# Mamba layer of a 12-layer kernel: projection in two halves, convolution halves in banks of their own, absolute value by ScalarE, the gate's Silu after the exponentials, last states in three pieces

## The chip, the cores and the metric
One core of a Trainium2 chip runs the whole program. The metric is the device time in microseconds, median of 3 runs. Engines: TensorE (PE; its weight loads are PEld), VectorE (DVE), ScalarE (ACT), GpSimd (POOL), SyncE (SP). Each has its own instruction queue, executed in order; they meet by semaphores.

## The reference, cut to what matters
The program is a stack of four groups of three layers on x of shape (2, 128, 256). The change touches the second layer only, a Mamba layer (b = 2, l = 128, 256 channels, 16 states, a convolution over 4 steps):

```python
xz = layernorm(x) @ W_in                      # 256 -> 512
xc, r = jnp.split(xz, 2, axis=-1)
xs = causal_conv(xc, conv_w) + conv_b         # 256 x 256 channels, 4 taps
u = silu(xs)
A = -jnp.exp(A_log)
dbc = u @ W_x                                 # 128 for dt, 16 for B, 16 for C
delta = softplus(dbc[..., :128] @ W_dt + b_dt)
deltaA = exp(delta * A)                       # per channel and state
deltaBu = delta * u * B
h = deltaA * h + deltaBu                      # scan over l
y = sum over states of h * C
out = (y + u * D) * silu(r)
x = x + out @ W_out + xs
```

## The kernel before, in words
Everything is written out by hand: for each layer a block with one function per engine, whose order is the order of its queue. A layer's block begins when all engines have left the one before it. The Mamba layer is `mamba_layer` (L806). Channels lie on partitions in two halves (c = 0, 1), the 256 columns are the 2 x 128 positions. PSUM is `ps`, 8 banks of 512 columns.

TensorE (L864 on): 14 filler matmuls that keep it active, the transposes of the normalised x, the projection W_in for four output groups (L873; groups 0 and 1, the convolution's input, in bank 0, groups 2 and 3, the gate's, in bank 1), one semaphore after all four. The convolution (L881) is 16 matmuls for each half, both halves in bank 2, one semaphore after both. Then w_x for dt (L887, bank 3) and for three copies of B and C (L891, 96 rows of bank 4), w_dt (L896, bank 7). An fp32 matmul is two instructions in the trace.

ScalarE (L946 on): copies the convolution's input out of bank 0 (L957), the gate's Silu (L960), Silu to u (L963), xs = the convolution plus its bias (L967), the copy of dt's input (L971), then Exp and Ln for softplus (L974, L976), and the exponentials of delta x A, 8 states for each of four units (L986), and then the absolute values of the next layer's weights with their sums (`sizes`, L1097). Dummy activations of one column (L952, L972, L977) bring a table in early. `ln_scalar` (L147) opens the next layer.

VectorE (L995 on): splits B and C into three bf16 parts (L1003 to L1007), so that 8 matmuls with a selecting matrix of ones (`spread`, L903) lay a row of B or C on all partitions. z = w_dt's result + b_dt (L1012), -|z| (L1016), and softplus(z) = max(z, 0) + log1p(exp(-|z|)), where log1p is a polynomial (L1019 to L1021) for small arguments and ScalarE's Ln elsewhere (L1023, L1024), added up in L1025 and L1026. z is then overwritten by delta x u (L1030). The four units are (states 0 to 7, c = 0), (0 to 7, c = 1), (8 to 15, c = 0), (8 to 15, c = 1). `inputs` (L1036) multiplies by B, `scan` (L1046) runs over positions, `times_c` (L1052) multiplies by C, `sums` on TensorE (L911) adds the 8 states of a unit with the identity matrix in PSUM, `gate` (L1058, L1060) adds u x D and multiplies by the gate, then TensorE applies W_out for each half (L936, L943) and adds xs by the identity (L939), and VectorE adds the result to x (L1081). The last unit's product is made in two pieces of 4 states.

POOL sets xcp's padding to zero (L851) and builds the selecting matrix (L855, L859); it is idle afterwards. SP only issues the load of a later layer's weights at the start of the block.

Of the kernel before, what the change touches and what calls it, by code (L numbers as in the profile page):

```python
# [22 lines left out]
P = 128  # L23
B = 2
# [781 lines left out]
def mamba_layer(k, name, slot, loaded, stage_loads):  # L806
# [7 lines left out]
    with ExitStack() as stack:  # L814
        def sb(nm, shape, dt=F32):
            return stack.enter_context(nc.sbuf_tensor(f"{name}_{nm}", shape, dt))
        s = semaphores(nc, stack, name, "a_capped pad_zero three_ready sel_ready xz_psum xc_ready conv_psum u_ready "
                 "dr_psum dr_ready bc_psum bc_split b_psum c_psum dz_psum dz_abs z_ready exp_ready log_ready a_exp a_ready "
# [14 lines left out]
        A = sb("A", [P, DC, MN])  # L833
        unused = sb("unused", [P, 1])
# [6 lines left out]
        high = ps[:, 4:8, :].rearrange("p a (r t) -> p (a r) t", r=2)  # L841
        units = [(half, c) for half in range(2) for c in range(DC)]

        with nc.Block() as block:
# [4 lines left out]
            @block.gpsimd  # L849
            def _(pool):  # L850
                nc.gpsimd.memset(xcp[:], 0.0).then_inc(s.pad_zero, 1)  # L851
                pool.wait_ge(s.pad_zero, 1)
                pool.wait_ge(g.xn_ready, n + 1)
                for i in range(3):
                    nc.gpsimd.tensor_copy(three[32 * i:32 * i + 32, :], k.identb[32 * i:32 * i + 32, 32 * i:32 * i + 32])\  # L855
                        .then_inc(s.three_ready, 1)
                    pool.wait_ge(s.three_ready, i + 1)

                nc.gpsimd.tensor_copy(sel, three[:].rearrange("p (n o) -> p n o", o=1)  # L859
                                      .broadcast_to([COPIES, 2 * MN, P])).then_inc(s.sel_ready, 1)  # L860

            @block.tensor
            def _(pe):
# [7 lines left out]
                for m in range(4):  # L871
                    for c in range(DC):
                        last = nc.tensor.matmul(ps[:, m // 2, (m % 2) * T:(m % 2 + 1) * T],  # L873
                                                w_in[:, c, m * P:(m + 1) * P], k.xnT[:, c, :],
                                                start=(c == 0), stop=(c == DC - 1))
                last.then_inc(s.xz_psum, 1)
                pe.wait_ge(s.xc_ready, 1)
                for m in range(DC):
                    for j in range(MK):
                        for c in range(DC):  # L880
                            last = nc.tensor.matmul(ps[:, 2, m * T:(m + 1) * T].rearrange("p (b t) -> p b t", b=B),  # L881
                                                    conv[:, j, c, m * P:(m + 1) * P], xcp[:, c, :, j:j + P],
                                                    start=(j == 0 and c == 0), stop=(j == MK - 1 and c == DC - 1))
                last.then_inc(s.conv_psum, 1)
                pe.wait_ge(s.u_ready, 1)
                for c in range(DC):
                    last = nc.tensor.matmul(ps[:, 3, 0:T], w_x[:, c, 0:MR], u[:, c, :],  # L887
                                            start=(c == 0), stop=(c == DC - 1))
# [9 lines left out]
                last.then_inc(s.dz_psum, 1)  # L898

# [15 lines left out]
                pe.wait_ge(s.bc_split, 1)  # L915
                pe.wait_ge(s.sel_ready, 1)
                spread(0, 0, s.b_psum)
# [11 lines left out]
                keep_busy(k, 5, 5)  # L929
                pe.wait_ge(s.hc_ready, 4)  # L930
                sums(3, 0, NHALF // 2)
                pe.wait_ge(s.hc_ready, 5)
                sums(3, NHALF // 2, NHALF).then_inc(s.y_psum, 1)
                pe.wait_ge(s.gated, 1)
                for b in range(B):
                    nc.tensor.matmul(ps[:, 4 + b, 0:D], z[:, 0, b * P:(b + 1) * P], w_out[:, 0, :],  # L936
                                     start=True, stop=False, skip_group_check=True)
                    for c in range(DC):
                        nc.tensor.matmul(ps[:, 4 + b, c * P:(c + 1) * P], xs[:, c, b * P:(b + 1) * P], k.ident[:],  # L939
                                         start=False, stop=False, skip_group_check=True)  # L940
# [6 lines left out]
            def _(act):  # L947
# [12 lines left out]
                nc.scalar.activation(flat(sr[:]), ps[:, 1, :], ACT.Silu, bias=k.zero[:])  # L960
                act.wait_ge(s.conv_psum, 1)
                for c in range(DC):
                    last = nc.scalar.activation(u[:, c, :], ps[:, 2, c * T:(c + 1) * T], ACT.Silu,  # L963
                                                bias=conv_b[:, c:c + 1])
                last.then_inc(s.u_ready, 1)
                for c in range(DC):
                    last = nc.scalar.activation(xs[:, c, :], ps[:, 2, c * T:(c + 1) * T], ACT.Identity,  # L967
                                                bias=conv_b[:, c:c + 1])
                last.then_inc(s.u_ready, 1)
                act.wait_ge(s.dr_psum, 1)  # L970
                nc.scalar.copy(dr, ps[:, 3, 0:T]).then_inc(s.dr_ready, 1)  # L971
                nc.scalar.activation(unused[:], k.zero[:], ACT.Exp, bias=k.zero[:])  # L972
                act.wait_ge(s.dz_abs, 1)
                nc.scalar.activation(ze, za, ACT.Exp, bias=k.zero[:]).then_inc(s.exp_ready, 1)  # L974
                act.wait_ge(s.exp_ready, 1)
                nc.scalar.activation(zl, ze, ACT.Ln, bias=k.ones[:, 0:1]).then_inc(s.log_ready, 1)  # L976
                nc.scalar.activation(unused[:], k.zero[:], ACT.Exp, bias=k.zero[:])  # L977
# [3 lines left out]
                for i, (half, c) in enumerate(units):  # L981
# [6 lines left out]
                    last.then_inc(s.dA_ready, 1)  # L988
                if k.following == "L0_ffn":
# [3 lines left out]
            def _(dve):  # L993
# [61 lines left out]
                def gate(c):  # L1055
# [3 lines left out]
                                                         ALU.mult, ALU.add))  # L1059
                    nc.vector.tensor_tensor(z[:, c, :], z[:, c, :], sr[:, c, :], ALU.mult).then_inc(s.gated, 1)  # L1060
# [14 lines left out]
                times_c(3, low, 0, NHALF // 2)  # L1075
                times_c(3, low, NHALF // 2, NHALF)
# [2462 lines left out]
```

## Time and profile before

| | us |
|---|---|
| median of 3 runs | 1417.43 |
| lowest and highest | 1414.89, 1417.97 |
| the profiled execution, its own time | 1408.27 |
| its span, first to last instruction | 1406.5 |
| the Mamba layer in it | 240.8 to 312.4 |
| mean granted TensorE clock | 0.964 of full |

The profile shows one execution. Its timeline gives for each merged stretch of instructions the start from the span's beginning, the duration, engine, source line, what is written from what, and in brackets how long the engine stood idle before it and who released it. Matmuls are pipelined: their durations contain the way to PSUM, and the distance of their starts is what they cost TensorE.

### The profile page before, as it was taken

The page shows a single profiled execution, that of the slowest core. Times are in us where ns is not written, and L with a number is a line of the kernel's source. Part 1 is how long each engine was busy: PE and PEld are TensorE (multiplying, and loading weights), DVE is VectorE, ACT ScalarE, POOL GpSimd, SP SyncE. Part 2 cuts the span into 40 slices and gives each one's busy share as a digit, 9 for nine tenths or more (in the row PEclk, how much of TensorE's full clock was granted, in tenths as well). Part 3 has the DMA queues.
Part 4 walks back from the last instruction along what each step waited for, and adds up shares of the span by engine and source line. Part 5 has one row for each costly group of instructions (what it writes and reads, how often), then busy time and mean ns, then how long its engine had stood idle before and what let it go on. Part 6 is the DMA issues. An engine that isn't in the chain of part 4 may idle for free. (4 is left out here: it accounts for less than half of the span.)

```text
span 1406.5 us, 25870 instructions
## 1 busy us (share of the span) xinstructions
PE 1231.5 (88%) x10035; PEld 846.6 (60%) x10035; DVE 1088.9 (77%) x2028; ACT 916.2 (65%) x1283; POOL 304.7 (22%) x235
## 2 busy tenths in 40 slices
PE   7999998478879888876989999978898899999987
PEld 3677776353335555555756766765685567666654
DVE  6877885686888999837488898955796798899564
ACT  5877775635667877732267777745695767677664
POOL 3000000001241110000006164250362063452400
PEclk9999999889999999988999999999999999999999
DMA  7999997001008999984169998950662889889700
GB/s 281 178 189 184 179 180 137 18 27 71 1 13 155 193 197 192 200 170 118 55 115 196 175 198 172 174 144 0 208 201 90 149 165 176 171 168 169 141 8 8
DMA packets 548587, 195.77 MB, mean 139 GB/s; under 512 B 534913, under 2 KB 535297, under 8 KB 546945
## 3 DMA queue, kind: packets, MB, share of 16 engines
q1 hardware_dynamic: 548480, 194.35, 69.0%
q8 instruction: 67, 1.10, 0.3%
q14 instruction: 40, 0.32, 0.1%
HBM read 59.83 MB, written 0.26 MB: 43 GB/s over the span
## 5 line engine op out<-in xcount | busy, mean ns | idle before, releaser
L729 DVE SCALAR_TENSOR_TENSOR arena<-L_xattn_sm,L_xattn_rr,arena 128x1024 f16<-128x1024 f32 x192 | 279.0, 1494 | 9.4 <-ACT arena L599 9.4
L460 PE MATMUL ps<-ctxT,L_xattn_qk 128*128 128x512 f16 x1152 | 265.5, 380 | 0.8 <-DVE L_xattn_mx L711 0.5
L584 ACT ACTIVATE L_xattn_sm<-L_xattn_sm,L_xattn_mx 128x2048 f32<-128x2048 f32 x96 | 192.2, 2002 | 78.9 <-DVE L_xattn_mx L711 78.1
L599 ACT ACTIVATE arena<-L_xattn_sm,L_xattn_rr 128x1024 f16<-128x1024 f32 x192 | 210.1, 1141 | 5.2
L474 PE MATMUL ps<-arena,ctx 128*128 128x128 f16 x2976 | 186.0, 222 | 18.4 <-DMA arena<-arena 18.3
L474 PEld LDWEIGHTS ps<-arena,ctx 128*128 128x128 f16 x2976 | 174.5, 99 | 33.1 <-DMA arena<-arena 22.6
L460 PEld LDWEIGHTS ps<-ctxT,L_xattn_qk 128*128 128x128 f16 x1152 | 111.1, 98 | 126.3 <-issue 3.2
L711 DVE CUSTOM_DVE_ANT_0 L_xattn_sm<-ps,L_xattn_bias 128x1024 f32<-128x1024 f32 x96 | 117.2, 1221 | 65.7 <-issue 65.4
L711 DVE CUSTOM_DVE_ANT_0 L_xattn_sm<-ps,L_xattn_bias,L_xattn_mx 128x1024 f32<-128x1024 f32 x96 | 123.2, 1284 | 1.0 <-issue 0.4
L484 PEld LDWEIGHTS ps<-arena,ctx 128*128 128x128 f16 x1488 | 90.8, 98 | 17.1
L484 PE MATMUL ps<-arena,ctx 128*128 128x128 f16 x1488 | 98.3, 219 | 0.0
L180 PE MATMUL ps<-ctxT,identh 128*128 128x512 f16 x328 | 86.9, 401 | 7.6 <-PEq L361 3.0
L2277 PE MATMUL ps<-arena 128*128 128x512 f16 x384 | 92.1, 391 | 0.0
L2289 PE MATMUL ps<-L_xattn_pt,arena 128*32 128x128 f16 x1024 | 70.4, 226 | 22.8 <-DMA L_xattn_pt<-L_xattn_pp 22.4
L2289 PEld LDWEIGHTS ps<-L_xattn_pt,arena 128*32 128x32 f16 x1024 | 59.9, 100 | 41.7 <-DMA L_xattn_pt<-L_xattn_pp 32.2
L589 ACT ACTIVATE L_xattn_rr<-L_xattn_raw,L_xattn_anyone 128x1 f32<-128x1 f32 x96 | 28.2, 293 | 85.8 <-DVE L_xattn_raw L721 84.9
L2419 ACT ACTIVATE L_xattn_pp<-L_xattn_sm,L_xattn_rr 128x1024 f16<-128x1024 f32 x64 | 70.0, 1140 | 20.8 <-DVE L_xattn_rr L2610 20.8
L2619 DVE SCALAR_TENSOR_TENSOR L_xattn_pp<-L_xattn_sm,L_xattn_rr,L_xattn_pp 128x1024 f16<-128x1024 f32 x64 | 79.6, 1285 | 2.7 <-ACT L_xattn_pp L2419 2.4
L2592 DVE CUSTOM_DVE_ANT_0 L_xattn_sm<-ps,arena 128x1024 f32<-128x1024 f32 x64 | 76.5, 1222 | 4.0 <-issue 3.7
L2407 ACT ACTIVATE L_xattn_sm<-L_xattn_sm,L_xattn_nm 128x2048 f32<-128x2048 f32 x32 | 64.1, 2002 | 19.1 <-DVE L_xattn_nm L2601 19.1
L2994 POOL TENSOR_TENSOR L_xattn_inv<-bits,L_xattn_exp 128x48 int32<-128x48 int32 x8 | 2.1, 264 | 304.9 <-DVE L_xattn_exp L2964 304.9
L2277 PEld LDWEIGHTS ps<-arena 128*128 128x128 f16 x384 | 36.2, 100 | 43.8 <-issue 5.1
(541 smaller groups left out, 2107.0 us busy)
## 6 DMA issues: line engine op xcount, KB each, us to landing
L_ffn_ring<-in_L_ffn_experts SPq DMA_DIRECT2D x34, 384.0 KB, 3.8
arena<-in_L_xattn_w SPq DMA_DIRECT2D x36, 320.0 KB, 4.0
arena<-in_L_ffn_experts SPq DMA_DIRECT2D x8, 768.0 KB, 8.7
arena<-in_L_xattn_w SPq DMA_DIRECT2D x6, 640.0 KB, 10.3
arena<-arena SPq DMA_TRANSPOSE x193, 4.5
arena<-in_L_ffn_codes SPq DMA_DIRECT2D x1, 3072.0 KB, 11.4
arena<-in_L_ffn_scales SPq DMA_DIRECT2D x8, 384.0 KB, 22.9
arena<-in_L_attn_w SPq DMA_DIRECT2D x1, 2163.0 KB, 19.2
```

The source lines that it names most:

```text
L180: k.nc.tensor.matmul(k.ps[:, bank, :], k.identh[:], k.ctxT[:, 0, 0, 0:512] if data is None else data, start=True, stop=True)
L460: last = nc.tensor.matmul(ps[:, at, :], qk[:, h // 2, qp, h % 2, b * P:(b + 1) * P], k.ctxT[:, cp, b, at * 512:(at + 1) * 512], start=(a = ...
L474: last = nc.tensor.matmul(O[h][:, b * P:(b + 1) * P], k.ctx[:, cp, b * KT + kt, :], pt[:, b, 0, kt, :], start=(kt == 0 and cp == 0), stop= ...
L484: last = nc.tensor.matmul(O[h][:, b * P:(b + 1) * P], k.ctx[:, 0, b * KT + kt, :], pt[:, b, 1, kt, :], start=False, stop=(kt == KT - 1), s ...
L584: nc.scalar.activation(sm[:, u % 2, :], sm[:, u % 2, :], ACT.Exp, bias=mx[:, u % 2, 1:2], scale=-1.0, accum_out=rs[:, u % 2:u % 2 + 1]).th ...
L599: nc.scalar.mul(pp[:, u % 2, 0, at], sm[:, u % 2, at], rr[:, u % 2:u % 2 + 1]).then_inc(s.p_high, 1)
L711: nc.vector.tensor_tensor_reduce(sm[:, u % 2, half * 1024:(half + 1) * 1024], ps[:, 2 * half:2 * half + 2, :].rearrange("p a n -> p (a n)" ...
L729: nc.vector.scalar_tensor_tensor(pp[:, u % 2, 1, at], sm[:, u % 2, at], rr[:, u % 2:u % 2 + 1], pp[:, u % 2, 0, at], ALU.mult, ALU.subtrac ...
L2277: last = nc.tensor.matmul(ps[:, at, :], qm[:, h % 4, qp, b * P:(b + 1) * P], knT[:, kp, h // 8, b, at * 512:(at + 1) * 512], start=(a == 0 ...
L2289: last = nc.tensor.matmul(O[h // 4][j:j + 32, b * P:(b + 1) * P], v[:, b * KT + kt, h, :, :].rearrange("p s d -> p (s d)"), pt[:, b, part, ...
L2592: nc.vector.tensor_tensor_reduce(sm[:, u % 2, half * 1024:(half + 1) * 1024], ps[:, 2 * half:2 * half + 2, :].rearrange("p a n -> p (a n)" ...
L2619: nc.vector.scalar_tensor_tensor(pp[:, u % 2, 1, at], sm[:, u % 2, at], rr[:, u % 2:u % 2 + 1], pp[:, u % 2, 0, at], ALU.mult, ALU.subtract)\
```

## The change
Six edits in one function; the number of multiplications and the results stay as they are.

1. `into` projects groups 0 and 1 (the convolution's input) first and signals; three filler matmuls follow. Groups 2 and 3 (the gate's) are projected after w_dt.
2. The convolution's halves go to banks 2 and 5 and signal one by one; Silu to u is signalled for each half, and w_x waits for each half by itself, after two fillers.
3. xs is made after Ln. The gate's half is copied raw to `sr` after that; its Silu comes after the exponentials, in place. The first spread waits for that copy (`gate_ready`, bank 1), `gate` for the Silu.
4. ScalarE makes |z| from w_dt's result with bias b_dt into a new tile `zm`; Exp takes scale -1. VectorE's z waits for it (same bank), L1016 goes.
5. POOL makes three of the five steps of B's and C's split. max(z, 0) + the polynomial is formed ahead of the wait for Ln.
6. xs is added in PSUM ahead of the last unit's sums, in place of five fillers. The last unit's product is in three pieces, of 2, 3 and 3 states.

```diff
...
+zm = sb("zm", [P, DC, T])
...
+CONV = (2, 5)
+LAST_STATES = ((0, 2), (2, 5), (5, NHALF))
...
+        pool.wait_ge(s.sel_ready, 1)
+        pool.wait_ge(s.bc_high, 2)
+        nc.gpsimd.tensor_copy(split[64:96, 1, :], rest[64:96, :]).then_inc(s.bc_parts, 1)
+        pool.wait_ge(s.bc_parts, 1)
+        nc.gpsimd.tensor_copy(split[32:64, 0, :], rest[32:64, :]).then_inc(s.bc_split, 1)
+        pool.wait_ge(s.bc_split, 1)
+        nc.gpsimd.tensor_tensor(split[64:96, 0, :], rest[64:96, :], split[64:96, 1, :], ALU.subtract)  .then_inc(s.bc_split, 1)
...
-        for m in range(4):
-            for c in range(DC):
-                last = nc.tensor.matmul(ps[:, m // 2, (m % 2) * T:(m % 2 + 1) * T],
-                                        w_in[:, c, m * P:(m + 1) * P], k.xnT[:, c, :],
-                                        start=(c == 0), stop=(c == DC - 1))
-        last.then_inc(s.xz_psum, 1)
+        def into(first, end):
+            for m in range(first, end):
+                for c in range(DC):
+                    last = nc.tensor.matmul(ps[:, m // 2, (m % 2) * T:(m % 2 + 1) * T],
+                                            w_in[:, c, m * P:(m + 1) * P], k.xnT[:, c, :],
+                                            start=(c == 0), stop=(c == DC - 1))
+            return last
+        into(0, 2).then_inc(s.xz_psum, 1)
+        keep_busy(k, 6, 3)
...
-                    last = nc.tensor.matmul(ps[:, 2, m * T:(m + 1) * T].rearrange("p (b t) -> p b t", b=B),
+                    last = nc.tensor.matmul(ps[:, CONV[m], 0:T].rearrange("p (b t) -> p b t", b=B),
...
-        last.then_inc(s.conv_psum, 1)
-        pe.wait_ge(s.u_ready, 1)
+            last.then_inc(s.conv_psum, 1)
+        keep_busy(k, 6, 2)
...
+            pe.wait_ge(s.u_ready, c + 1)
...
+        into(2, 4).then_inc(s.gate_psum, 1)
...
-        pe.wait_ge(s.bc_split, 1)
+        pe.wait_ge(s.bc_split, 2)
...
+        pe.wait_ge(s.gate_ready, 1)
...
-        keep_busy(k, 5, 5)
-        pe.wait_ge(s.hc_ready, 4)
-        sums(3, 0, NHALF // 2)
-        pe.wait_ge(s.hc_ready, 5)
-        sums(3, NHALF // 2, NHALF).then_inc(s.y_psum, 1)
-        pe.wait_ge(s.gated, 1)
-        for b in range(B):
-            nc.tensor.matmul(ps[:, 4 + b, 0:D], z[:, 0, b * P:(b + 1) * P], w_out[:, 0, :],
-                             start=True, stop=False, skip_group_check=True)
+        pe.wait_ge(s.u_ready, 3)
+        for b in range(B):
...
-                                 start=False, stop=False, skip_group_check=True)
+                                 start=(c == 0), stop=False, skip_group_check=True)
+        for i, (first, end) in enumerate(LAST_STATES):
+            pe.wait_ge(s.hc_ready, 4 + i)
+            last = sums(3, first, end)
+        last.then_inc(s.y_psum, 1)
+        pe.wait_ge(s.gated, 1)
+        for b in range(B):
+            nc.tensor.matmul(ps[:, 4 + b, 0:D], z[:, 0, b * P:(b + 1) * P], w_out[:, 0, :],
+                             start=False, stop=False, skip_group_check=True)
...
-        nc.scalar.activation(flat(sr[:]), ps[:, 1, :], ACT.Silu, bias=k.zero[:])
-        act.wait_ge(s.conv_psum, 1)
...
-            last = nc.scalar.activation(u[:, c, :], ps[:, 2, c * T:(c + 1) * T], ACT.Silu,
-                                        bias=conv_b[:, c:c + 1])
-        last.then_inc(s.u_ready, 1)
-        for c in range(DC):
-            last = nc.scalar.activation(xs[:, c, :], ps[:, 2, c * T:(c + 1) * T], ACT.Identity,
-                                        bias=conv_b[:, c:c + 1])
-        last.then_inc(s.u_ready, 1)
+            act.wait_ge(s.conv_psum, c + 1)
+            nc.scalar.activation(u[:, c, :], ps[:, CONV[c], 0:T], ACT.Silu, bias=conv_b[:, c:c + 1])\
+                .then_inc(s.u_ready, 1)
...
+        act.wait_ge(s.dz_psum, 1)
+        for c in range(DC):
+            last = nc.scalar.activation(zm[:, c, :], ps[:, 7, c * T:(c + 1) * T], ACT.Abs, bias=b_dt[:, c:c + 1])
+        last.then_inc(s.dz_abs, 1)
...
-        nc.scalar.activation(ze, za, ACT.Exp, bias=k.zero[:]).then_inc(s.exp_ready, 1)
+        nc.scalar.activation(ze, flat(zm[:]), ACT.Exp, bias=k.zero[:], scale=-1.0).then_inc(s.exp_ready, 1)
...
+        for c in range(DC):
+            last = nc.scalar.activation(xs[:, c, :], ps[:, CONV[c], 0:T], ACT.Identity,
+                                        bias=conv_b[:, c:c + 1])
+        last.then_inc(s.u_ready, 1)
+        act.wait_ge(s.gate_psum, 1)
+        nc.scalar.copy(flat(sr[:]), ps[:, 1, :]).then_inc(s.gate_ready, 1)
...
+        act.wait_ge(s.gate_ready, 1)
+        nc.scalar.activation(flat(sr[:]), flat(sr[:]), ACT.Silu, bias=k.zero[:]).then_inc(s.gate_silu, 1)
...
-        chain(nc.vector.tensor_copy(split[:, 0, :], ps[0:COPIES, 4, 0:T]))
-        chain(nc.vector.tensor_tensor(rest, ps[0:COPIES, 4, 0:T], split[:, 0, :], ALU.subtract))
-        nc.vector.tensor_copy(split[32:64, 0, :], rest[32:64, :])
-        chain(nc.vector.tensor_copy(split[64:96, 1, :], rest[64:96, :]))
-        nc.vector.tensor_tensor(split[64:96, 0, :], rest[64:96, :], split[64:96, 1, :], ALU.subtract)\
-            .then_inc(s.bc_split, 1)
-        dve.wait_ge(s.dz_psum, 1)
+        nc.vector.tensor_copy(split[:, 0, :], ps[0:COPIES, 4, 0:T]).then_inc(s.bc_high, 1)
+        dve.wait_ge(s.bc_high, 1)
+        nc.vector.tensor_tensor(rest, ps[0:COPIES, 4, 0:T], split[:, 0, :], ALU.subtract).then_inc(s.bc_high, 1)
+        dve.wait_ge(s.dz_abs, 1)
...
-        dve.wait_ge(s.z_ready, 1)
-        nc.vector.scalar_tensor_tensor(za, flat(z[:]), -1.0, flat(z[:]), ALU.mult, ALU.min)\
-            .then_inc(s.dz_abs, 1)
...
+        dve.wait_ge(s.z_ready, 1)
+        nc.vector.scalar_tensor_tensor(flat(delta[:]), flat(z[:]), 0.0, za, ALU.max, ALU.add)
...
-        chain(nc.vector.tensor_tensor(zl, zl, za, ALU.add))
-        nc.vector.scalar_tensor_tensor(flat(delta[:]), flat(z[:]), 0.0, zl, ALU.max, ALU.add)\
+        nc.vector.tensor_tensor(flat(delta[:]), flat(delta[:]), zl, ALU.add)\
...
-        dve.wait_ge(s.u_ready, 1)
+        dve.wait_ge(s.u_ready, 2)
...
+            dve.wait_ge(s.gate_silu, 1)
...
-        times_c(3, low, 0, NHALF // 2)
-        times_c(3, low, NHALF // 2, NHALF)
+        for first, end in LAST_STATES:
+            times_c(3, low, first, end)
...
```

## Rows read from the trace of the kernel before

**Rows 1.** The page: busy us (share of the span) and instructions of each engine.
```profile
PE 1231.5 (88%) x10035; PEld 846.6 (60%) x10035; DVE 1088.9 (77%) x2028; ACT 916.2 (65%) x1283; POOL 304.7 (22%) x235
```

**Rows 2.** Busy time of each engine in a stretch of the layer; PEclk is the granted clock.
```profile
266.90:290.00 23.10, 3.77 (x13) 2.57 (x14) 22.79 (x14) 20.70 (x38) 0.00 (x0) 0.51 0.00 1
```

**Rows 3.** Timeline, opening of the layer: start us, us, engine, line, form, count, [idle before, releaser].
```profile
245.24 3.69 PE L873 MATMUL ps<-xnT,arena 128*128 128x256 f32 x16 [0.77 <-ACT xnT L196]
...
248.04 0.29 ACT L952 ACTIVATE L_attn_unused<-zero 128x1 f32<-128x1 f32 x1
...
249.01 0.65 ACT L957 COPY L_attn_xcp<-ps 128x256 f32<-128x256 f32 x2 [0.68 <-issue]
...
249.71 7.17 PE L881 MATMUL ps<-L_attn_xcp,arena 128*128 128x256 f32 x32 [0.78 <-ACT L_attn_xcp L957]
...
256.92 0.84 ACT L963 ACTIVATE L_attn_u<-ps,arena 128x256 f32<-128x256 f32 x2 [6.67 <-PE ps L881]
...
258.98 0.37 ACT L971 COPY L_attn_h<-ps 128x256 f32<-128x256 f32 x1 [0.49 <-PE ps L887]
...
259.64 1.03 PE L896 MATMUL ps<-L_attn_h,arena 128*128 128x256 f32 x4
```

**Rows 4.** Timeline, from the splits to the first inputs; ScalarE to the next layer's weights.
```profile
260.30 0.42 DVE L1004 TENSOR_TENSOR L_attn_h<-ps,L_attn_split 96x256 f32<-96x256 f32 x1
...
261.81 0.87 DVE L1012 TENSOR_SCALAR L_attn_z<-ps,arena 128x256 f32<-128x256 f32 x2
...
263.45 0.72 ACT L974 ACTIVATE L_attn_h<-L_attn_h,zero 128x512 f32<-128x512 f32 x1 [2.49 <-DVE L_attn_h L1016]
...
264.19 1.28 ACT L976 ACT_TABLE_LOAD   x1
...
265.48 0.72 ACT L976 ACTIVATE L_attn_h<-L_attn_h,ones 128x512 f32<-128x512 f32 x1
...
269.21 0.69 DVE L1030 TENSOR_TENSOR L_attn_z<-L_attn_delta,L_attn_u 128x512 f32<-128x512 f32 x1
...
269.27 15.84 ACT L986 ACTIVATE arena<-L_attn_delta,zero,L_attn_A 128x256 f32<-128x256 f32 x32 [1.46 <-DVE L_attn_delta L1026]
...
269.94 4.49 DVE L1036 TENSOR_TENSOR L_attn_h<-L_attn_z,ps 128x2048 f32<-128x2048 f32 x2
...
285.01 1.99 ACT L1097 ACTIVATE arena<-arena,zero 128x2048 bf16<-128x2048 f32 x1
```

**Rows 5.** Timeline of TensorE: the spreads of B and C.
```profile
261.84 1.95 PE L903 MATMUL ps<-L_attn_split,arena 96*128 96x256 bf16 x16 [1.17 <-DVE L_attn_split L1007]
...
274.48 1.89 PE L903 MATMUL ps<-L_attn_split,arena 96*128 96x256 bf16 x8 [10.69 <-DVE L_attn_h L1036]
```

**Rows 6.** Granted clock, in stretches of 2 us.
```profile
266.00:268.00 2.00, 0.00 (x0) 0.00 (x0) 1.71 (x4) 1.78 (x3) 0.00 (x0) 0.86 0.00 0
...
290.00:292.00 2.00, 2.00 (x8) 1.65 (x7) 2.00 (x2) 0.00 (x0) 0.00 (x0) 0.67 0.00 0
```

**Rows 7.** Groups of POOL by form: shapes and count | busy us, mean ns | idle before.
```profile
L1945 POOL TENSOR_TENSOR L_ffn_ap<-L_ffn_av,L_ffn_ap 128x256 f16<-128x256 f32 x34 | 23.1, 679 | 32.3 <-ACT L_ffn_ap L1910 32.3
```

**Rows 8.** Timeline, from the last product by C to the next layer.
```profile
303.80 2.35 DVE L1052 TENSOR_TENSOR L_attn_h<-L_attn_h,ps 128x1024 f32<-128x1024 f32 x2
...
305.07 3.72 PE L911 MATMUL ps<-L_attn_h,ident 128*128 128x256 f32 x16 [0.95 <-DVE L_attn_h L1052]
...
308.83 0.48 DVE L1058 SCALAR_TENSOR_TENSOR L_attn_z<-L_attn_u,arena,ps 128x256 f32<-128x256 f32 x1 [1.83 <-PE ps L911]
...
309.35 0.42 DVE L1060 TENSOR_TENSOR L_attn_z<-L_attn_z,L_attn_sr 128x256 f32<-128x256 f32 x1
...
310.38 1.03 PE L943 MATMUL ps<-arena,L_attn_z 128*128 128x256 f32 x4
...
311.02 0.92 DVE L1081 TENSOR_TENSOR x<-x,ps 128x256 f32<-128x256 f32 x2 [1.25 <-PE ps L943]
...
312.43 1.28 ACT L147 ACT_TABLE_LOAD   x1 [23.35 <-PEq L844]
```

More of the change, by code:

```diff
@@ L816, in sb @@
             return stack.enter_context(nc.sbuf_tensor(f"{name}_{nm}", shape, dt))
-        s = semaphores(nc, stack, name, "a_capped pad_zero three_ready sel_ready xz_psum xc_ready conv_psum u_ready "
-                 "dr_psum dr_ready bc_psum bc_split b_psum c_psum dz_psum dz_abs z_ready exp_ready log_ready a_exp a_ready "
+        s = semaphores(nc, stack, name, "a_capped pad_zero three_ready sel_ready xz_psum gate_psum xc_ready conv_psum u_ready "
+                 "dr_psum dr_ready gate_ready gate_silu bc_psum bc_high bc_parts bc_split b_psum c_psum dz_psum dz_abs z_ready exp_ready log_ready a_exp a_ready "
                  "delta_ready dA_ready dBu_ready scan_done hc_ready y_psum gated out_psum", k.turns[slot])
@@ L928, in _ @@
                 sums(2, 0, NHALF).then_inc(s.y_psum, 1)
-                keep_busy(k, 5, 5)
-                pe.wait_ge(s.hc_ready, 4)
-                sums(3, 0, NHALF // 2)
-                pe.wait_ge(s.hc_ready, 5)
-                sums(3, NHALF // 2, NHALF).then_inc(s.y_psum, 1)
+                pe.wait_ge(s.u_ready, 3)
+                for b in range(B):
+                    for c in range(DC):
+                        nc.tensor.matmul(ps[:, 4 + b, c * P:(c + 1) * P], xs[:, c, b * P:(b + 1) * P], k.ident[:],
+                                         start=(c == 0), stop=False, skip_group_check=True)
[3 more added lines that the diff above has]
+                last.then_inc(s.y_psum, 1)
                 pe.wait_ge(s.gated, 1)
@@ L936, in _ @@
                     nc.tensor.matmul(ps[:, 4 + b, 0:D], z[:, 0, b * P:(b + 1) * P], w_out[:, 0, :],
-                                     start=True, stop=False, skip_group_check=True)
-                    for c in range(DC):
-                        nc.tensor.matmul(ps[:, 4 + b, c * P:(c + 1) * P], xs[:, c, b * P:(b + 1) * P], k.ident[:],
-                                         start=False, stop=False, skip_group_check=True)
+                                     start=False, stop=False, skip_group_check=True)
                 pe.wait_ge(s.gated, 2)
@@ L959, in _ @@
                 last.then_inc(s.xc_ready, 1)
-                nc.scalar.activation(flat(sr[:]), ps[:, 1, :], ACT.Silu, bias=k.zero[:])
-                act.wait_ge(s.conv_psum, 1)
                 for c in range(DC):
-                    last = nc.scalar.activation(u[:, c, :], ps[:, 2, c * T:(c + 1) * T], ACT.Silu,
-                                                bias=conv_b[:, c:c + 1])
-                last.then_inc(s.u_ready, 1)
-                for c in range(DC):
-                    last = nc.scalar.activation(xs[:, c, :], ps[:, 2, c * T:(c + 1) * T], ACT.Identity,
-                                                bias=conv_b[:, c:c + 1])
-                last.then_inc(s.u_ready, 1)
+                    act.wait_ge(s.conv_psum, c + 1)
+                    nc.scalar.activation(u[:, c, :], ps[:, CONV[c], 0:T], ACT.Silu, bias=conv_b[:, c:c + 1])\
+                        .then_inc(s.u_ready, 1)
                 act.wait_ge(s.dr_psum, 1)
@@ L972, in _ @@
                 nc.scalar.activation(unused[:], k.zero[:], ACT.Exp, bias=k.zero[:])
+                act.wait_ge(s.dz_psum, 1)
+                for c in range(DC):
+                    last = nc.scalar.activation(zm[:, c, :], ps[:, 7, c * T:(c + 1) * T], ACT.Abs, bias=b_dt[:, c:c + 1])
+                last.then_inc(s.dz_abs, 1)
                 act.wait_ge(s.dz_abs, 1)
-                nc.scalar.activation(ze, za, ACT.Exp, bias=k.zero[:]).then_inc(s.exp_ready, 1)
+                nc.scalar.activation(ze, flat(zm[:]), ACT.Exp, bias=k.zero[:], scale=-1.0).then_inc(s.exp_ready, 1)
                 act.wait_ge(s.exp_ready, 1)
                 nc.scalar.activation(zl, ze, ACT.Ln, bias=k.ones[:, 0:1]).then_inc(s.log_ready, 1)
+                for c in range(DC):
+                    last = nc.scalar.activation(xs[:, c, :], ps[:, CONV[c], 0:T], ACT.Identity,
[3 more added lines that the diff above has]
+                nc.scalar.copy(flat(sr[:]), ps[:, 1, :]).then_inc(s.gate_ready, 1)
                 nc.scalar.activation(unused[:], k.zero[:], ACT.Exp, bias=k.zero[:])
```

## Prediction

> **What bounds the kernel now.** The page's busy shares come first: TensorE 88%, VectorE 77%, ScalarE 65% of 1406.5 us [rows 1]. They average twelve layers, and the change touches one, so what decides is the timeline of that layer, from 240.8 to 312.4 us. Read so, it has three parts. From 240.8 to 269.9 it is one chain of dependent steps that passes from engine to engine; each waits for the one before [rows 3, 4]. From 269.94 to 306.1 VectorE is the bound: in a stretch of 23.10 us it is busy 22.79 [rows 2], and nothing of that work is changed. From 306.1 to 311.94 it is a chain again [rows 8]. A gain in the first and third part moves the end of the layer one for one, because blocks follow each other in order and the next one opens at 312.43 [rows 8], waiting for this one. Times below are on the clock of this trace.
>
> **Convolution's half first.** The 8 projection matmuls (16 instructions) take 3.69 from 245.24 [rows 3]. Half of them end near 245.24 + 8 x 0.22 + 0.2 = 247.2. ScalarE is then not free: its table load and dummy end at 248.33 [rows 3]. So the copy starts at 248.35, not 249.01: 0.66 gained, the rest of the 1.8 is lost behind ScalarE. The three filler matmuls end near 247.7, before the copies (about 249.0), and are free. Below nothing isn't likely; above, 1.8 isn't to be had.
>
> **Halves in own banks.** The convolution takes 7.17 as before [rows 3], now from 249.05 to 256.22. Before, both Silus (0.84) follow its end at 256.88, two w_x matmuls follow them, and the copy of their result begins at 258.98 [rows 3]. Now the first Silu lies under the second half, and the first w_x matmul runs beside the second Silu. TensorE issues the last convolution matmul by 256.02, two fillers 0.43, the first w_x matmul 0.43: 256.88. The second Silu ends at 256.26 + 0.47 = 256.73. The second w_x matmul follows at 256.88 and lands 0.6 later (two of this size take 1.03 with their landing, 0.43 apart), so the copy begins at 257.55: 1.43 in all, 0.77 of it from this part. If the fillers were absent it would be 0.1 more.
>
> **Absolute value by ScalarE, split by POOL.** w_dt's matmuls land at 259.24 instead of 260.67 [rows 3]. ScalarE has copied dr (0.37) by 257.92, loads the Exp table (1.28) and runs its dummy (0.29, as at 248.04) until 259.53. Two Abs of 128x256 from PSUM with a bias have no row; the nearest is the pair of Silus, 0.84, with a bias too. They end at 260.35, Exp (0.72) at 261.12. Before, Exp ended at 264.17, since VectorE was at the splits until 261.8, then took 0.87 for z and 0.7 for the absolute value [rows 4]. So Exp ends 3.05 earlier. I call its end E. Bounds of the Abs pair: 0.65 (the copies of 2 x 256) to 1.0.
>
> **The polynomial.** Before, z = delta x u ends 5.73 after E (264.17 to 269.90) [rows 4], over eight VectorE steps and 0.23 of waiting for Ln. After, there are again eight (one goes ahead of the wait, none goes): 5.50. But z itself now waits for the Abs pair (they share a bank) and ends at 260.37 + 0.87 = 261.25, 0.13 after E. So z = delta x u ends at E + 5.6 = 266.7, and the first inputs follow there, not at 269.94: **3.2 us** to here.
>
> **What is late next there.** Three things could be.
> - The spread of B waits for the gate's copy now. On ScalarE behind E: table load and Ln to E + 2.02 [rows 4], the two xs activations 0.84 (as the Silus), the copy of 512 columns 0.6 (as the pair of copies, 0.65 [rows 3]): E + 3.5. TensorE then needs 8 matmuls: 1.1 at full clock (16 took 1.95), 1.89 at half [rows 5]. B is there at E + 4.6 or E + 5.4, against E + 5.6. Hidden, at half clock by 0.2 only; gone, each tenth costs a tenth, and I allow 0.8.
> - The exponentials of A x delta: delta is ready at E + 4.9, but the second Exp table and dummy (1.6) end at E + 5.1. All 32 take 15.84, so the first eight 4.0 [rows 4] to E + 9.1; VectorE is at its inputs (4.49) until E + 10.1. Hidden by 1.0.
> - POOL's split: VectorE's two steps end at 260.72 - 1.44 = 259.3 [rows 4]; three POOL operations on 32 x 256. The nearest row is 0.68 for 128 x 256 with two inputs [rows 7], so 1.7 with their waits, done by 261.0. TensorE wants them at E + 3.5 = 264.6. So each of the three may take 1.7, two and a half times that row for a quarter of its partitions, before it costs anything.
>
> The moved second half of the projection (1.8 on TensorE, 259.0 to 260.9) stands ahead of the spread only, which waits longer anyway. The gate's Silu with its table load (1.28 + 0.7) lies behind the exponentials, ahead of the next layer's weight sums; ScalarE stood idle 23.35 us before the next layer [rows 8]. Both cost nothing.
>
> **The clock there.** TensorE is idle from 260.9 to 264.6 now. In the trace it ended work at 263.8 [rows 5] and the granted clock fell from 1.00 to 0.50 (2.4 to 1.2 GHz) within 266 to 268 [rows 6]. The new gap is about as long as that stretch was, so the spread may run at the lower level, and I took the 1.89 in judging it. The Trainium skill ("TensorE: Matmul & The Clock Gate", the HAM clock gate) says that the chip's watch on TensorE's activity runs free of the kernel, so that the moment of a change differs from run to run. By it B comes at E + 4.6 or E + 5.4 by chance, and the sum stays; one trace cannot show the scatter.
>
> **Table switches.** A table load starts at 264.19 and Ln at 265.48: 1.30 for all of it [rows 4]. The Trainium skill ("ScalarE: Activation LUTs", What ACT_TABLE_LOAD costs) puts a drain of 1.38 us on top of each switch. By that figure Exp ends 1.4 later, B comes 1.2 late and the first exponentials another 0.6 behind it: a gain near 1.0; this trace shows no such gap (0.01 us from the end of the load to Ln), so I count it as a rival only.
>
> **The tail.** The last product by C is cut 2, 3, 3 states instead of 4, 4. One of 1024 elements is ready 1.2 after 303.80, and TensorE starts at 305.07 [rows 8]. With 512 elements (2.35/2048 each, 0.59, and 0.1 fixed: 0.68) it starts at 304.53. The 8 sums need 3.72 without a gap, the pieces come at 304.5, 305.35 and 306.2, each before it is needed: 308.25 instead of 308.79. Then gate(1), 0.48 + 0.42 [rows 8], to 309.23. Before, gate(1) was done at 309.77 but TensorE, with w_out and the xs product for both batches in its queue, began the last matmuls at 310.27 to 310.38; now xs is summed ahead (0.9, in place of five fillers, done by 303.9) and they begin at 309.28. Their result is added from 0.72 later, 0.92: 310.92 instead of 311.94. **1.0 us.** Bounds: 0.5 (only the piece) to 1.2.
>
> **Sum.** 3.2 + 1.0 = 4.2 us, 0.30%. The profiled execution took 1408.27 (span 1406.5), so it would take 1404.1. The median of the runs, 1417.43, is 9.2 above it for reasons outside the kernel's steps; I take the difference over: 1413.2.
>
> **Rivals.**
> - *The gate's copy decides.* B is late instead of z: the ScalarE run E + 3.5 is longer by a table load for Identity or Copy behind Ln (1.28), and TensorE is at half clock. For it: half clock leaves 0.2. Against it: the copy at 249.01 follows Silu's table without a load of its own [rows 3]. B at E + 6.7, 1.1 late: gain 3.1, time 1414.3.
> - *No difference.* Abs wants a table of its own, and Exp has to be loaded again: 2 x 1.3 on the chain, beside the 1.1 above: gain 0.5, time 1416.9. Against: the absolute values of the next layer's weights (285.01) follow the last exponential with no load and no gap [rows 4]. A dead time behind each table load would end in the same place: of 1.3 us each it would leave 1.1; the row has 0.01. I give it 0.01 of the chance below.
> - *Slower: the clock doesn't come back.* Place: the sums over states. TensorE starts them at half clock; in the trace it regained full clock within 290 to 292 [rows 6], while the first sums ran without a gap, and then the sums kept pace. If the phase after the change misses this burst, each sum takes 16 x 0.44 = 7 us instead of 3.7. TensorE, from 284.9: sums 7, spread 1.9, sums 7 and 7 to 307.8, xs 1.8, last sums 7 to 316.6, gate 0.9, last matmuls and additions 2.6: near 320, 8 us late: 1425. It decides only if the clock is still low when the third sum begins; a rise up to 3 us later is hidden. Against: the sums that lifted the clock are as many and as dense as before.
> - *The change doesn't do what it says*: TensorE falls to half clock in the gap of 1.35 before the convolution (0.78 before). 3 us of convolution at half clock lose 1.5: gain 2.7, 1414.7. Against: after 263.8 the clock was still full at 266 [rows 5, 6], after a longer gap.
>
> **Chances.** Forecast 0.66, gate's copy 0.13, early clock 0.05, no difference 0.11, slower 0.05. The comparison can't tell less than 0.2% (2.8 us) from nothing, and three runs of before lie 3.1 us apart, so a part of the first three counts as same. Faster 0.74, same 0.21, slower 0.05. The forecast's own range is 1411.8 to 1414.6; with the neighbours and the drift of medians 1410.0 to 1417.0.
>
> **What would show it.** In the profile after: xcp copies near 248.35 with the convolution 0.1 later; Exp's end near 261.1; first inputs within 0.3 of 266.7 and no idle time of VectorE before them on TensorE's spread; POOL's three operations done before 262; no table load beside Abs, Identity or Copy; 33.8 us from the first inputs to the end of the last scan, as before; from there to the last addition 7.2 where it was 8.2. It is wrong if VectorE waits for the spread by over 0.5, if the layer is shortened by under 3 us, or if the rest of the kernel moves by more than 1 us.

## The result, and the profile after

| | before | after |
|---|---|---|
| median of 20 runs each, us | 1418.09 | 1411.24 |
| lowest to highest | 1414.89 to 1422.89 | 1404.33 to 1416.37 |
| profiled execution, its span | 1408.27, 1406.5 | 1408.90, 1407.2 |
| Mamba layer in it | 71.68 | 67.12 |

The ratio of the comparison is 0.9941, interval 0.993 to 0.9953: 8.4 us, twice the 4.2 forecast. (The means of these runs are 8.1 apart, their medians 6.9.) Three later comparisons of the same two kernels gave 0.9967, 0.9957 and 0.9957. The two profiled executions differ by 0.6 us the other way, though the layer is 4.56 shorter: the other eleven layers took 1340.0 against 1334.8. So two questions are to be kept apart: what the layer gives, and what the kernel gives beyond it.

A layer's length here is the distance of the first row of its layer norm (L123) to the next layer's. The timeline after, with the lines that answer to [rows 3, 4, 5 and 8]:

```profile
241.04 0.75 DVE L123 BATCH_NORM_STATS2 stats<-x 128x6 f32<-128x256 f32 x2 [0.53 <-PEq L361]
...
245.43 1.97 PE L884 MATMUL ps<-xnT,arena 128*128 128x256 f32 x8 [0.77 <-ACT xnT L196]
...
246.96 1.19 DVE L1024 TENSOR_SCALAR L_attn_A<-L_attn_A 128x32 f32<-128x32 f32 x1 [3.29 <-ACT L_attn_A L969]
...
248.24 0.29 ACT L970 ACTIVATE L_attn_unused<-zero 128x1 f32<-128x1 f32 x1
...
248.44 0.63 ACT L975 COPY L_attn_xcp<-ps 128x256 f32<-128x256 f32 x2
...
249.12 7.17 PE L895 MATMUL ps<-L_attn_xcp,arena 128*128 128x256 f32 x32 [1.07 <-ACT L_attn_xcp L975]
...
256.33 0.47 ACT L980 ACTIVATE L_attn_u<-ps,arena 128x256 f32<-128x256 f32 x1 [2.98 <-PE ps L895]
...
257.62 0.37 ACT L983 COPY L_attn_h<-ps 128x256 f32<-128x256 f32 x1 [0.82 <-PE ps L902]
...
259.51 0.82 ACT L987 ACTIVATE L_attn_zm<-ps,arena 128x256 f32<-128x256 f32 x2
...
260.36 0.72 ACT L990 ACTIVATE L_attn_h<-L_attn_zm,zero 128x512 f32<-128x512 f32 x1
...
260.43 0.67 POOL L870 TENSOR_TENSOR L_attn_split<-L_attn_h,L_attn_split 32x256 bf16<-32x256 f32 x1
...
263.74 0.58 ACT L998 COPY L_attn_sr<-ps 128x512 f32<-128x512 f32 x1
...
264.46 3.53 PE L919 MATMUL ps<-L_attn_split,arena 96*128 96x256 bf16 x16 [3.42 <-ACT L_attn_sr L998]
...
265.84 0.69 DVE L1049 TENSOR_TENSOR L_attn_z<-L_attn_delta,L_attn_u 128x512 f32<-128x512 f32 x1
...
266.57 4.49 DVE L1055 TENSOR_TENSOR L_attn_h<-L_attn_z,ps 128x2048 f32<-128x2048 f32 x2
...
281.75 1.28 ACT L1012 ACT_TABLE_LOAD   x1
...
299.51 1.05 PE L949 MATMUL ps<-ident,L_attn_xs 128*128 128x128 f32 x8
...
300.42 2.42 DVE L1071 TENSOR_TENSOR L_attn_h<-L_attn_h,ps 128x512 f32<-128x512 f32 x3
...
301.17 3.72 PE L927 MATMUL ps<-L_attn_h,ident 128*128 128x256 f32 x16 [0.60 <-DVE L_attn_h L1071]
...
305.92 1.13 PE L961 MATMUL ps<-arena,L_attn_z 128*128 128x256 f32 x4 [0.17 <-DVE L_attn_z L1080]
...
306.66 0.92 DVE L1101 TENSOR_TENSOR x<-x,ps 128x256 f32<-128x256 f32 x2 [0.79 <-PE ps L961]
...
308.16 0.43 DVE L123 BATCH_NORM_STATS2 stats<-x 128x6 f32<-128x256 f32 x1
```

Both clocks begin at a layer's first row, 240.84 before and 241.04 after. The convolution starts 8.08 into the layer, was 8.87; the copy of dt's input 16.58, was 18.14; Exp ends at 20.04, was 23.33; the inputs start at 25.53, were 29.10. From the first inputs to the end of the last scan it is 33.81, was 33.82. The last addition ends 7.2 behind that scan, was 8.18. VectorE stands idle nowhere between z and the inputs, B's spread included: the spread is at half clock (264.46, 16 matmuls in 3.53, where the same 16 took 1.95 before), and the eighth of its matmuls, which completes B, ends at 266.29, 0.28 before the inputs start. In the third and fourth profile of the changed kernel the same eight were issued in 0.76 and not 1.40, so at full clock, and the layer took 67.11 and 67.13 all the same: B is hidden at either clock, by chance the one or the other, as forecast. No table load stands beside Abs, Identity or Copy.

### The profile page after: what moved, and what is told of

Read it like the earlier page. It is cut to its first block and busy times, and to the rows that moved or that the text cites. A ratio compares the mean times of both kernels' runs of the same rounds, so it can differ in the third digit from the quotient of the medians.

```text
span 1407.2 us, 25877 instructions
## 1 busy us (share of the span) xinstructions
PE 1236.8 (88%) x10035; PEld 850.4 (60%) x10035; DVE 1086.2 (77%) x2025; ACT 918.9 (65%) x1287; POOL 306.5 (22%) x238
```

## The experiments

A diff is against the changed kernel where nothing else is said. Each ratio is to the kernel before, run on the same chip. Experiments of one session share their runs of before (the second comparison, the kernel before against itself, the delay and the late exponential; the third comparison, the absolute value on VectorE and the two first versions with seven fillers; the fourth comparison and the last version; the front and the tail), so their ratios are not independent of each other. "Give or take" means a 95% interval.

**Cut behind three layers.** Both kernels with

```diff
-RUN = tuple(range(12))
+RUN = tuple(range(3))
```

> The kernel before, ended behind its third layer (layers 0 to 2 of 12; the other nine are left out, so the output is that of three layers). It is the base for the next run. Layer theory (the extra gain is in the Mamba layer, whose state in the profiled execution was a lucky one): its times scatter by 3 us or more, and in its profile the Mamba layer takes more than 72.5. Later-layers theory: they scatter by under 1.5 us and the layer takes 71.6 +- 0.5.

> The changed kernel, ended behind its third layer in the same way. Layer theory: 6.5 to 9 us faster than the short kernel before. Later-layers theory (the layer gives what its two profiles show, 71.68 - 67.12 = 4.56, and the rest comes behind it): 4.0 to 5.0 faster, with up to 0.9 taken by the third layer where it falls to half clock.

Medians of 5 runs: 340.63 and 336.55, 4.1 us apart (means 4.5, give or take 2.2). In the profiles the layer takes 71.68 and 67.12, to the hundredth as in the whole kernels. The short kernel before spreads over 5.0 us (338.57 to 343.58), as the layer theory had it and the other had not; but its layer is no longer than in the first profile, and 6.5 to 9 us are not there. The layer theory falls: nothing hidden in the layer gives 8.

**The front alone, the tail alone.** The front is the changed kernel with the old tail; the tail alone is the kernel before with the new one (the last diff lines of the change).

> All edits but the tail: xs is added behind the gates as before, five fillers, two pieces of four states. By the two traces the Mamba layer takes 71.68 - 3.56 = 68.1. If the rest of the kernel is not moved by it: 3.6 faster than before (ratio 0.9975). If later layers give as well: 5 or more (0.9965 or less).

> The tail alone: xs ahead of the last sums, no fillers, last product in pieces of 2, 3 and 3 states; everything ahead as before. By the traces the layer takes 71.68 - 0.99 = 70.7, and the kernel is 1.0 faster (ratio 0.9993). If it is the missing part that brings the rest: 3 or more (0.998 or less).

0.9978 (0.996 to 0.9996), 3.1 us, and 0.9983 (0.9964 to 1.0002), 2.4 us: neither is told from its 3.6 and 1.0. But the layers took 69.80 and 72.39, each 1.68 more than expected. TensorE's timeline of the front kernel shows where:

```profile
242.75 4.87 PE L876 MATMUL ps<-ctxT,identh 128*128 128x512 f16 x14 [1.27 <-PEq L361]
...
247.45 0.60 PE L190 MATMUL ps<-ident,xn 128*128 128x128 f32 x4
```

The 14 opening fillers took 4.87, not 3.18, and the transposes came 4.7 into the layer, not 3.0. That code is the same in all kernels. Less 1.68 both layers are as the traces said: 68.12 and 70.71.

**The kernel before against itself, and the change again.**

> The kernel before once more, against itself: what two medians of one kernel differ by. Both theories: ratio 1.000, within 0.0015. In its profile the Mamba layer takes 71.68, or 71.68 + 1.68 = 73.36 if its 14 opening fillers run at half clock as in the two partial kernels.

> The changed kernel once more. Layer-only theory (the change gives what its layer shows, 4.56, and the first comparison had 3 to 4 of scatter on top): 3.5 to 6 faster, ratio 0.9958 to 0.9975. Later-layers theory (the kernel behind the layer gains as well): 7 to 10 faster again, ratio 0.993 to 0.995. Profile: Mamba layer 67.12 or 68.80.

1.0008 (0.9995 to 1.0022), and 0.9967 (0.9952 to 0.9981), 4.7 us. The layers: 73.38 and 68.81, both with the slow opening, and again 4.57 apart. The granted clock and TensorE in the opening of the kernel before, this time:

```profile
242.00:244.00 2.00, 0.85 (x4) 0.40 (x3) 0.69 (x1) 0.00 (x0) 0.00 (x0) 1.00 0.00 0
...
244.00:246.00 2.00, 1.88 (x6) 0.77 (x7) 1.42 (x7) 1.58 (x2) 0.54 (x1) 0.65 0.55 123
...
246.00:248.00 2.00, 2.00 (x6) 0.70 (x5) 0.74 (x3) 0.00 (x0) 1.02 (x4) 0.50 0.87 344
...
248.00:250.00 2.00, 1.42 (x9) 0.75 (x7) 0.00 (x0) 0.54 (x1) 2.00 (x1) 1.00 0.97 401
```

```profile
244.12 4.87 PE L866 MATMUL ps<-ctxT,identh 128*128 128x512 f16 x14 [1.27 <-PEq L361]
...
248.82 0.60 PE L190 MATMUL ps<-ident,xn 128*128 128x128 f32 x4
```

TensorE is thinly used at the end of the layer before (0.85 of 2 us). The clock falls to 0.50 (1.2 GHz) near 244.6 (a mean of 0.65 in 244 to 246) and is back at 1.00 at 248; in the first profile of before the same stretch stayed at 1.00. Whether it falls differs between executions of one kernel.

**Later layers moved back.** At the end of the layer, with TensorE busy beside it:

```diff
+                keep_busy(k, 6, 18)
...
+                spare = h[:, 0, :, :].rearrange("p n t -> p (n t)")
+                chain(nc.vector.tensor_tensor_scan(spare, dA[:, 0, :, :].rearrange("p n t -> p (n t)"), spare, 0.0,
+                                                   ALU.mult, ALU.add))
```

> The changed kernel with 4.5 us of work more at the end of the Mamba layer (one more scan on VectorE, whose result nobody uses, and 18 fillers beside it on TensorE), so that all later layers start where they do in the kernel before. Layer-only theory: 4.5 slower than the changed kernel, so equal to before within 1.5 (ratio 0.999 to 1.001). Later-layers theory by content: 2.5 to 4 faster than before (0.9972 to 0.9982); by position (later layers fare better when they start earlier): equal to before.

1.0004 (0.999 to 1.0017): the delay takes all back. The layer took 73.27, that is 67.12, 1.69 for the slow opening, and 4.46 for the delay (the scan's row is 4.42). So the change's content, apart from the time it saves, gives nothing that this can show: by content alone the ratio would be 0.9972 to 0.9982. It says less on an effect of the later layers' position, since in the same session the change itself gave 4.7 us, and 0.1 of extra gain is nothing to take back.

**The change, third and fourth time.**

> The changed kernel a third time, since the first comparison (0.9941) and the second (0.9967) differ by more than their scatter. Layer-only theory: 4.6 faster again, ratio 0.9955 to 0.998, and its Mamba layer takes 67.12 or 68.80. Later-layers theory: 0.9945 or less.

> The changed kernel a fourth time. Scatter theory: 0.9955 to 0.998 (4.56 us is 0.9968), which draws the average of the four towards 0.9957. Later-layers theory, with layers 8 to 12 as the place: 0.995 or less.

0.9957 (0.9935 to 0.9978) and 0.9957 (0.9938 to 0.9975), 6.1 us each; layers 67.11 and 67.13. Weighted by the inverse squares of their intervals the four comparisons average 0.9953, give or take 0.0008: 6.7 us, of which the layer has 4.56. The three that came after the first, which had raised the question, average 0.9962, give or take 0.0010: 5.4 us, and that holds the layer's 4.56.

**Cut behind four and behind seven layers** (`RUN` as above, 4 and 7).

> The kernel before, ended behind its fourth layer (layers 0 to 3; the other eight are left out). Base for the next; its profile: Mamba layer 71.68 or 73.38.

> The changed kernel, ended in the same place. Scatter theory: 4.0 to 5.2 faster than the short kernel before, as at three layers (4.1 by medians, 4.5 by means). Later-layers theory with the fine attention layer as the place: 6 or more.

> The kernel before, ended behind its seventh layer (layers 0 to 6; the other five are left out). Base for the next.

> The changed kernel, ended in the same place. Scatter theory: 3.5 to 5.7 faster. Later-layers theory with the three layers in between as the place: 6 to 7.5 faster.

Medians 617.16 and 612.10; 945.67 and 942.97. By means of the five runs each: 4.2 and 4.0 us apart, after 4.5 at three layers (give or take 3.5, 3.3 and 2.2). No growth with the layers is seen as far as seven, but 2 us of it would not be seen either.

**The absolute value on VectorE again**, the split left with POOL:

```diff
-        for c in range(DC):
-            last = nc.scalar.activation(zm[:, c, :], ps[:, 7, c * T:(c + 1) * T], ACT.Abs, bias=b_dt[:, c:c + 1])
...
+        nc.vector.scalar_tensor_tensor(za, flat(z[:]), -1.0, flat(z[:]), ALU.mult, ALU.min).then_inc(s.dz_abs, 1)
```

> The changed kernel with -|z| on VectorE again, everything else as changed (the split stays with POOL, so VectorE is free for z when w_dt's matmuls land). It tells the two halves of that edit apart. z and -|z| then take 0.88 + 0.03 + 0.69 = 1.60 ahead of Exp, where the Abs pair takes 0.85 with ScalarE's dummy ending 0.1 after the landing: Exp ends 0.5 later, z is there at once; Mamba layer 67.12 + 0.5 = 67.6 (or 69.3). So the POOL split, not Abs, would carry 1.6 of the 2.1 gained between w_dt and Exp. If the absolute value on ScalarE carries most: 68.5 or more (70.2).

```profile
261.88 0.88 DVE L1029 TENSOR_SCALAR L_attn_z<-ps,arena 128x256 f32<-128x256 f32 x2
...
262.79 0.69 DVE L1033 SCALAR_TENSOR_TENSOR L_attn_h<-L_attn_z 128x512 f32<-128x512 f32 x1
...
262.96 1.04 POOL L870 TENSOR_TENSOR L_attn_split<-L_attn_h,L_attn_split 32x256 bf16<-32x256 f32 x1
...
263.52 0.72 ACT L986 ACTIVATE L_attn_h<-L_attn_h,zero 128x512 f32<-128x512 f32 x1 [1.38 <-DVE L_attn_h L1033]
```

0.997 (0.9951 to 0.9989). Layer 67.72, with the opening at full clock: given POOL's split, Abs on ScalarE carries 0.6. The other 1.1 of the 1.7 gained there is put down to VectorE freed from the split; no run has Abs on ScalarE and the split on VectorE.

**A's exponential late.**

```diff
-        act.wait_ge(s.a_capped, 1)
-        nc.scalar.activation(A[:], A[:], ACT.Exp, bias=k.zero[:]).then_inc(s.a_exp, 1)
         nc.scalar.activation(unused[:], k.zero[:], ACT.Silu, bias=k.zero[:])
...
         nc.scalar.copy(dr, ps[:, 3, 0:T]).then_inc(s.dr_ready, 1)
-        nc.scalar.activation(unused[:], k.zero[:], ACT.Exp, bias=k.zero[:])
+        act.wait_ge(s.a_capped, 1)
+        nc.scalar.activation(A[:], A[:], ACT.Exp, bias=k.zero[:]).then_inc(s.a_exp, 1)
```

> The changed kernel, with A's exponential made behind the copy of dt's input, in place of the dummy that brings Exp's table, and its sign on VectorE while that waits for the absolute values. It takes one table load and one activation (1.28 + 0.32) from ScalarE ahead of the convolution's input: that copy starts when the projection lands, near 247.2 on the changed kernel's clock, not at 248.44. Expected: Mamba layer 67.12 - 1.1 = 66.0 (or 67.7 with half-clock fillers), 1.1 faster than the changed kernel. Against it: TensorE's fillers end at 247.8 and the convolution can't start sooner.

Layer 67.89, that is 66.20 with 1.69 for the slow opening: 0.92 better. The ratio, 0.9971 (0.9952 to 0.9989), can't show it.

**Seven opening fillers, alone and with it.** `range(14)` becomes `range(7)`.

> The changed kernel with 7 opening fillers instead of 14. At half clock 14 take 4.87 and hold the transposes, which need xn at 3.03 behind the layer's start; 7 take 3.0. Expected: Mamba layer 67.1 at full clock as before, 67.12 + 0.2 to 0.7 instead of + 1.69 where the opening is at half clock (transposes at half clock themselves), on average 0.5 to 1 faster than the changed kernel. Against it: TensorE is less busy in the opening, the clock falls more often or rises later, and the projection and convolution run at half clock: + 2 or more.

> The changed kernel with both: A's exponential late, and 7 opening fillers. Expected: Mamba layer 66.2 at full clock (the trace of the late exponential alone has 67.89, that is 66.20 + 1.69), 66.4 to 66.9 at half clock; the kernel 5.5 to 6.5 faster than before (ratio 0.9955 to 0.996), the fastest of all.

> The changed kernel with A's exponential late and 7 opening fillers, again. By its trace (66.29 at half clock against 68.80) it should be 0.8 to 2.5 faster than the changed kernel on the same chip; last time it was 1.3 faster by means. Half-clock opening: 66.3 again; full clock: 65.6 to 66.0.

Seven alone: 0.9943 (0.9922 to 0.9964), layer 66.74. Both: 0.9944 (0.9923 to 0.9966), layer 66.29, and again 0.9929 (0.9908 to 0.9949), layer 66.35. TensorE with seven alone (full clock), and in the second profile of the version with both (half clock):

```profile
244.55 1.67 PE L876 MATMUL ps<-ctxT,identh 128*128 128x512 f16 x7 [1.27 <-PEq L361]
...
247.13 0.66 PE L190 MATMUL ps<-ident,xn 128*128 128x128 f32 x4 [0.92 <-DVE xn L139]
```

```profile
244.25 2.91 PE L876 MATMUL ps<-ctxT,identh 128*128 128x512 f16 x7 [1.27 <-PEq L361]
...
246.95 1.06 PE L190 MATMUL ps<-ident,xn 128*128 128x128 f32 x4
```

At full clock (1.67) the transposes wait for xn and not for fillers: 14 of them had held them by 0.4 in the good case too, which I had not expected. At half clock (2.91) the layer is 66.35 where 14 fillers make it 67.89. The version with both has the lowest ratios: its two average 0.9936, 9 us, against 0.9953 for the change. The two intervals overlap, so between the versions it is the layer's lengths that show the difference: at half clock 66.3 against 68.8. (At full clock the changed kernel has 67.1; the version with both has no profile there.)

## Why the prediction was wrong

**The layer: right in mechanism, 8% small.** Forecast 4.2, found 4.56. By its terms:

| step | forecast | found |
|---|---|---|
| convolution's half first | 0.66 | 0.79 |
| halves in own banks | 0.77 | 0.77 |
| Abs by ScalarE, split by POOL | 1.62 | 1.73 |
| polynomial to the first inputs | 0.13 | 0.28 |
| scans and products | 0 | 0.01 |
| tail | 1.0 | 0.98 |

The missing 0.4 is one habit: I set each step at the end of the one before, but neighbours on one engine of which the second doesn't need the first's result overlap by 0.09. The copy starts at 248.44, before its dummy's end (248.53); Abs at 259.51, before its own dummy's end; VectorE's polynomial begins (261.15) before z's row ends (261.24), and the step behind max(z, 0) + the polynomial (263.67) before that ends (263.75). Four such joints on the path make 0.35, about what is missing. The Trainium skill ("ScalarE: Activation LUTs", What ACT_TABLE_LOAD costs) says that ACTIVATEs back to back overlap by some 93 ns, and this trace agrees; I had read it for the drain and not for this.

**What I called hidden was hidden.** B came 0.3 ahead of need with the spread at half clock; 0.2 was worked out. POOL's split was done at 261.10, forecast 261.0. The exponentials began 0.1 late and had 1.1 of slack (the first eight end at 269.94, the scan starts at 271.12). ScalarE's late Silu was followed by the weight sums, and still stood idle 20 us. The cost of Abs, taken from the Silu pair (0.84), was 0.82.

**The sum: this step failed.** "I take the difference over" set the kernel's gain equal to one layer's in one pair of profiles, with the rest unmoved to 1 us, and put the 9.2 us between that profile and the median down to "reasons outside the kernel's steps". They lie inside its steps. The second profile of the same kernel (1419.28) is 11.0 above the first, 1.7 of it in the Mamba layer and 9.3 in the other eleven. Over 14 profiles of whole kernels, which share all code but this layer's, those eleven took 1334.8 to 1349.9 us, and the profile I started from had the lowest. The first layer alone, which runs ahead of the change, took 240.8 to 244.7.

What moves them, at the places looked at, is how long TensorE is granted half clock; and over the 14 profiles the whole time of the eleven layers goes with their time at half clock (79 to 109 us; correlation 0.91), which fits but doesn't show the cause of each swing. The opening of the Mamba layer is one place (1.69). The fifth layer (20.38 or 22.07) has the same step, its 13 opening fillers 2.97 or 4.65. The last layer took 55.67 in the first profile of before and 58.95 in the second; ten us of each, 3 us behind the layer's start:

```profile
1353.80:1363.80 10.00, 9.86 (x50) 6.15 (x48) 7.03 (x32) 7.43 (x20) 0.00 (x0) 1.00 0.00 0
```

```profile
1361.60:1371.60 10.00, 10.00 (x32) 7.85 (x31) 5.74 (x31) 6.15 (x17) 0.00 (x0) 0.53 0.01 2
```

The third layer (26.7, and in three of the 14 profiles 27.6 to 27.7) is another. In the profile after, one row of 8 of its matmuls took 3.50 at a clock of 0.69 and 0.50; in the profile before, 1.90 at 1.00. TensorE's row before and after, and the clock after:

```profile
320.25 1.90 PE L1153 MATMUL ps<-L_ffn_wq,L_ffn_xqT 128*128 128x512 bf16 x8 [1.07 <-ACT L_ffn_xqT L1192]
```

```profile
315.88 3.50 PE L1173 MATMUL ps<-L_ffn_wq,L_ffn_xqT 128*128 128x512 bf16 x8 [1.08 <-ACT L_ffn_xqT L1212]
```

```profile
315.00:317.00 2.00, 1.12 (x3) 0.43 (x4) 0.00 (x0) 0.83 (x2) 0.00 (x0) 0.69 0.30 123
...
317.00:319.00 2.00, 2.00 (x6) 0.76 (x5) 0.38 (x1) 1.89 (x3) 0.00 (x0) 0.50 0.03 8
```

Larger swings lie in the attention layers (the fourth took 265.7 to 271.9). They too go with the time at half clock (correlation 0.76 in the fourth), but the rows in which they arise were not looked up. So a profile's span minus its layer says nothing of the median, and the range needed two parts: the layer's, narrow, and the scatter of the comparison itself, whose first draw was 8.4 where the average of four is 6.7.

**What stays open.** The average exceeds the layer by 2.1 us, about 1.1 either way, and more than half of that comes from the first comparison (without it: 0.9, give or take 1.4). The excess is not in the layer: every pair of profiles with the same opening has 4.55 to 4.58. The granted clock, which is on record for each execution, takes off a part more. In the 111 runs of before in the later sessions an execution's time goes with its time at half clock, twice the missing share of the clock times the time (correlation 0.85, 0.26 us for each us). An estimate at equal clock, by one line through all whole-kernel runs of these sessions (a level for each session and each version), makes the change worth 5.6 us in the three later comparisons, give or take 0.6; the 20 runs of the first lie 6.2 below the same line, the clocks of their partners not being on record. By that estimate about 1 us is left over the layer's 4.56, and the delayed kernel, which has the change's content, keeps nothing of it (1.2 slower than before, give or take 1.0): that speaks for the earlier start of the later layers and against content, and no more. Which layer that 1 us would be in, and why, no run here tells. Of the rivals none came: no late B, no own table for Abs, no clock that stays low, none that falls ahead of the convolution (7.17 as before). The dead time behind a table load didn't come either: Ln at 262.40 follows the load at 261.10 (1.28) by 0.02.

## What to carry to other kernels

Work out a change in a serial stretch by the joints of the chain, with the overlap of neighbours at each, and forecast the stretch; then ask separately how much the rest of the kernel differs between executions of the same code. Take the length of the stretch from the profiles as the measurement, comparing profiles with the same clock in it, since it repeated to 0.02 us, when single runs of the kernel scatter by 2 to 3 (standard deviation). Where the granted clock of every execution is at hand, set the times beside it before looking for a cause in the code. Fillers that keep TensorE's clock up must end before the step they stand ahead of even at half clock: their number is set by the slower level.

## What the runs showed of the hardware

- Whether the granted clock falls in a thin stretch differs between executions of one kernel; here it moved the layer by 1.69. It was low in the opening in 11 of 20 profiles. Less the opening, the changed kernel's layer was the same to 0.02.
- POOL and VectorE hold each other up. The 32x256 subtraction on POOL took 0.67 in the changed kernel, beside VectorE reading PSUM (260.36), and 1.04 beside VectorE's -|z| with two inputs in SBUF (262.79 in its fence); 0.66 to 0.67 in all other profiles that have it. VectorE's sign of A (128x32) took 1.19 while POOL wrote the selecting matrix (246.96 above), and ended 0.05 after POOL's copy did; with seven fillers alone it started 0.4 earlier, took 1.57 and ended at the same place, so it was held until POOL's copy was done. POOL's copy took 3.59 in every case. In the front kernel, where the sign came after it, it took 0.18, as in the seven other profiles with 14 fillers and the slow opening that have it in this place:

```profile
250.34 0.18 DVE L1023 TENSOR_SCALAR L_attn_A<-L_attn_A 128x32 f32<-128x32 f32 x1 [4.97 <-ACT L_attn_A L968]
```

The Trainium skill ("GPSIMD Engine Reference", Specifications) says that POOL's interface to SBUF is shared with VectorE and contended by VectorE's instructions with two SBUF inputs or in a two-port mode; the first pair of numbers agrees. The change put POOL's split there with 3 us of slack, so it cost nothing.
